# Issuing the stores of gathered blocks' results from ACT in place of SP

## What is computed

```python
x = layernorm(x + attn(x))        # attention in windows of 128 tokens over this and the previous window, v = k
x = layernorm(x + ffn(x))
# ffn: rotary positions, then causal attention over 2048 tokens, 16 heads of 16
q, k, v = q_in @ Wq.T + bq, k_in @ Wk.T + bk, x @ Wv.T + bv
attn = softmax(where(causal, q @ k.T / 4, -inf)); ctx = attn @ v
x1 = layer_norm(x + ctx @ out_proj_w.T + out_proj_b, ln1)
gates = softmax(x1 @ gate_w.T + gate_b); top_gates, top_idx = top_k(gates, 2)   # 8 experts
moe_out = sum of the two chosen (x1 @ expert_w[e].T + expert_b[e]) * gate
return layer_norm(x1 + moe_out, ln2)
```

## Time and profile before

| | |
|---|---|
| time, median of 3 runs | 1423.48 us (1422.62 to 1425.06) |
| the profiled execution | 1425.19 us, its span 1423.5 us |
| busy share of PE, DVE, ACT, POOL | 94%, 75%, 57%, 40% |
| granted TensorE clock, mean | 0.977 of 2.4 GHz |
| bytes moved | 140.77 MB, mean 99 GB/s |
| transfers issued by SP | all but the gathers and scatters of Pool |

### The profile page before, as it was taken

The page is one execution under the profiler, slowest core; times in us unless marked ns, Lnnn a source line. Parts: engine busy times, 40 slices in busy tenths (PEclk is TensorE's granted clock), DMA queues, the critical chain, the costliest instruction groups (busy, mean ns, idle before and its releaser), DMA issues. The chain is left out here.

```text
span 1423.5 us, 29390 instructions
## 1 busy us (share of the span) xinstructions
PE 1334.6 (94%) x9678; PEld 766.4 (54%) x9678; DVE 1072.4 (75%) x2782; ACT 805.4 (57%) x1749; POOL 572.1 (40%) x806
## 2 busy tenths in 40 slices
PE   8889899999999999999979888999999999999984
PEld 6767655545554453556656545665433445665441
DVE  3665877987888977674559977786999886666776
ACT  3235366556666567676745455656656666666541
POOL 4434422221221532223558645343454023322786
PEclk9999999999999999999989999999989999999996
DMA  3765432232111423445375543554432123443331
GB/s 113 191 179 130 123 79 62 62 91 57 40 40 47 95 58 92 110 117 147 89 181 135 133 85 74 163 166 136 109 77 63 29 48 67 131 125 104 89 73 46
DMA packets 221665, 140.77 MB, mean 99 GB/s; under 512 B 130246, under 2 KB 215934, under 8 KB 221259
## 3 DMA queue, kind: packets, MB, share of 16 engines
q1 hardware_dynamic: 209755, 123.50, 32.7%
q0 software_dynamic: 11760, 15.40, 5.6%
HBM read 97.35 MB, written 40.88 MB: 97 GB/s over the span
## 5 line engine op out<-in xcount | busy, mean ns | idle before, releaser
L1320 DVE TENSOR_REDUCE mxs<-bank 128x1 f32<-128x512 f32 (+3 forms) x1120 | 712.5, 667 | 169.2 <-PE bank L1753 95.6
L1213 ACT ACTIVATE pbuf<-bank 128x512 f32<-128x512 f32 (+1 forms) x1112 | 599.0, 593 | 296.3 <-PE bank L1804 187.7
L1781 PE MATMUL bank<-qs,ks 99*128 99x256 bf16 (+3 forms) x1536 | 426.5, 321 | 16.4 <-DVE rD L1445 6.8
L1753 PE MATMUL bank<-ks,qs 96*128 96x512 bf16 (+3 forms) x1280 | 423.3, 351 | 4.0 <-DVE mxs L1320 1.3
L1804 PE MATMUL bank<-pbuf,vcur 128*17 128x256 f32 (+3 forms) x3072 | 274.0, 474 | 9.1 <-DMA vcur<-v_scratch 7.0
L1781 PEld LDWEIGHTS bank<-qs,ks 99*128 99x128 bf16 x1536 | 142.2, 98 | 192.0 <-issue 69.4
L1753 PEld LDWEIGHTS bank<-ks,qs 96*128 96x128 bf16 x1280 | 123.1, 98 | 111.3 <-issue 21.3
L1804 PEld LDWEIGHTS bank<-pbuf,vcur 128*17 128x17 f32 x3072 | 70.8, 97 | 140.1 <-issue 97.4
L1125 POOL DMA_INDIRECT gathering<-x_scratch,gathering x69 | 68.3, 990 | 182.1 <-PE bank L1928 158.5
L1136 POOL DMA_INDIRECT gathering<-ys_scratch,gathering x48 | 78.8, 1641 | 46.9 <-issue 18.1
L1079 POOL CAST parts<-qkf 128x512 bf16<-128x512 f32 x28 | 17.7, 632 | 175.3 <-DVE qkf L1414 175.2
(11 more groups left out here) (334 smaller groups left out, 1941.6 us busy)
## 6 DMA issues: line engine op xcount, KB each, us to landing
gathering<-exp_t SPq DMA_DIRECT2D x69, 256.0 KB
vcur<-v_scratch SPq DMA_DIRECT2D x92, 136.0 KB, 2.8
parts_scratch<-parts SPq DMA_DIRECT2D x29, 384.0 KB, 3.4
ys_scratch<-gathering SPq DMA_DIRECT2D x69, 128.0 KB, 3.2
xw<-windows SPq DMA_DIRECT2D x29, 256.0 KB, 3.4
x_scratch<-x SPq DMA_DIRECT2D x53, 128.0 KB, 2.4
qs<-parts_scratch SPq DMA_DIRECT2D x32, 192.0 KB, 3.8
ks<-parts_scratch SPq DMA_DIRECT2D x28, 192.0 KB, 3.8
```

The lines of the kernel that those rows point to most:

```text
L1213: nc.scalar.activation(pbuf[:, u0:u0 + heads, nj * P - cols:nj * P], bk[:, 0:heads * cols].rearrange("p (h t) -> p h t", h=heads), ACT.Exp)\
L1320: v.reduce_max(mxs[:, j * HJ + h:j * HJ + h + heads, c], bk[:, 0:heads * cols].rearrange("p (h t) -> p h t", h=heads), AX_X)\
L1753: last = mm(bk[:, x * cols:(x + 1) * cols].rearrange("p (n t) -> p n t", t=P), qs6[0:KR, pos % QRING, head // HJ, j, head % HJ, :], ks5[0: ...
L1781: last = mm(bk[:, x * cols:(x + 1) * cols].rearrange("p (n t) -> p n t", t=P), ks5[0:KR + NPART, kslot, kb % GT, head, :], qs6[0:KR + NPAR ...
```

## The change

The step `s_st` moves from SP to ACT: the same transfer of the same slot to the same place, with the same semaphore, is issued in ACT's stream. There it waits until ACT's own `s_ec` has finished. In the planner its engine becomes ACT, its cost 150 ns in place of 900, it loses the 640 ns (5 x 128) of wire and SP's settling of 1700 ns, and gains 3000 ns in `INDIRECT` and ACT's settling of 150.

```diff
-INDIRECT = {"s_g": 3600, "b_g1": 4000, "b_g2": 5000, "t_sc": 3600}
+INDIRECT = {"s_g": 3600, "b_g1": 4000, "b_g2": 5000, "t_sc": 3600, "s_st": 3000}
...
-                    add("s_st", u + x, "SP", 900, ("s_ec", u + x))
+                    add("s_st", u + x, "ACT", 150, ("s_ec", u + x))
...
-                elif name == "s_st":
-                    u, t = T, T % BLOCKS
-                    sp.wait_ge(*drain("s_e", u))
-                    sp.dma_start(ys_dram[u // BLOCKS][t * P:(t + 1) * P, :], yslot[u % 2]).then_inc(yslot_stored[u % 2], 16)
...
+                elif name == "s_st":
+                    u, t = T, T % BLOCKS
+                    act.wait_ge(*drain("s_e", u))
+                    act.dma_start(ys_dram[u // BLOCKS][t * P:(t + 1) * P, :], yslot[u % 2]).then_inc(yslot_stored[u % 2], 16)
```

## The result

The changed kernel takes 1430.49 us by the median of 18 runs (1424.7 to 1436.47), the kernel before 1423.05 in 18 runs of its own (1416.98 to 1428.59). The ratio is 1.0048, with a 95% interval of 1.0033 to 1.0064: slower by 7 us. The profiled execution took 1428.72 us with a span of 1427.0, the one of before 1425.19 with 1423.5. So the two traces show 3.5 us of the 7; single executions of one kernel lie up to 0.4% from its median, so a difference of a few us between two whole traces may be chance.

A forecast was written before the change was run, and what follows sets the result against it. The prediction took TensorE, busy 94% of the span, to bound the kernel. Its terms, 0 + 0 + 2 + 0 = +2 us, gave 1425.5 us from a usual run's 1423.5; the range was 1414 to 1436.

The forecast's parts named there:

- What bounds the kernel: TensorE, busy 94% of the span; only 3.1 us idle in the three store phases; gain taken as 0, at most −3.1.
- its part of the chain: In the chain that ended last, TensorE's part ends at 1336.1 us; what follows is Pool's with DVE's.
- The landing: Stores land after 3.2 us, 1.7 without a load before; up to 1.5 us gain at phase ends, taken as 0.
- What comes to ACT: ACT's time for issuing 69 stores: from nothing to 42 us, against 148.5 us of its idle time in the phases.
- The upper end of 0.61 us a store: ACT's most for each store: 0.11 us of lost overlap, 0.03 for the semaphore, 0.47 for the issue.
- The 12 us pushed back: ACT time delayed by the 69 stores: half at 0.1 us each, half at 0.26 us each.
- What reaches TensorE: Of the 12 us pushed back on ACT, one part in six delays TensorE: +2 us.
- first rival: ACT's slip empties the three `st` banks, whose cover is 0.3 us, and reaches TensorE: 10 us, 1433.5 us; chance 0.25.
- The order: New planner costs change bank hand-out and all five engines' orders after about 545 us: 0, with −8 to +8 us.
- third rival: The new order makes one more long wait of TensorE: +7 us, 1430.5 us; chance 0.10.
- The sign that I gave for the order: TensorE's idle changing by more than 5 us in 686 to 856 or behind 1312 us would show the order.

The follow-up runs named there:

- e8: Changed kernel with ACT's list swapped at 30 places, so one activation stands between copy and store; 1428.94 us, ratio 1.0040 to the kernel before.
- e1: Changed kernel with the planner of the kernel before: old order and banks, the 69 stores issued by ACT; 1426.79 us, ratio 0.9995.
- e12: e1 with the planner's cost of a store 800 in place of 900 ns, giving e11's order with stores on ACT; 1456.57 us, ratio 0.9989.
- e11: Kernel before, stores still on SP, only the planner's cost of a store set to 800 in place of 900 ns; 1418.96 us, ratio 0.9969.
- e6: Order of the kernel before, stores issued by ACT in two halves of 64 partitions each; 1479.4 us, ratio 1.0130.
- e9: Changed kernel, but the planner gets the new costs for the third chunk's stores alone; 1429.13 us, ratio 1.0030 to the kernel before.
- e10: Changed kernel, but the planner gets the new costs for the first two chunks' stores alone; 1427.49 us, ratio 1.0031 to the kernel before.
- e3: Changed kernel with the store's landing in the planner 3100 in place of 3000 ns, another order; 1433.74 us, ratio 1.0054.
- e2: Kernel before with the changed kernel's planner: new order and banks, stores still issued by SP; 1428.13 us, ratio 1.0014.
- e4: The changed kernel itself, run again on another chip beside e5; 1465.24 us, ratio 1.0044 to the kernel before.
- e5: The same kernel as e2 (new order, stores on SP), run again beside the changed kernel; 1462.18 us, ratio 1.0032.

## Why the prediction was right in its range and not in its likeliest case

I forecast 1425.5 us as the likeliest and no change as the likeliest of the three, with 1414 to 1436 as the range and 0.35 for slower. It came out at 1430.5, which is slower, above the 1426.3 at which I let no change end. Step by step:

- **What bounds the kernel.** Right for the phases with the stores: they have 3.1 us of idle to give, and nothing was given (3.6 us now). No run shows a gain from SP's freed time or the earlier landing. Wrong for the end: I let TensorE end at 1336 us, where its part of the chain ends. But it is busy for 82.05 us of the last 112, and its last matmul ends at 1404.7, so the last stage had TensorE's work in it for the new order to move.
- **The landing.** The open question, 3.2 us or 1.7, is answered: 1.8 where ACT issues, 3.2 where SP does, in both orders. The stores had stood behind the 256 KB of weights ahead of them. The rule of the Trainium skill ("DMA: Bandwidth & Descriptors", section "Issuing engines are not separate DMA queues"), that transfers of different issuers run on the same 16 DMA engines and a second issuer saves only the sequencer's time, fits e8: a store on ACT's own queue right behind the weights lands after 3.2 us as well. What I drew from it, a gain of 0, was wrong: the 1.4 us come from the store being started ahead of the load. That nobody waits for it was right as far as the times show.
- **What comes to ACT.** The upper end of 0.61 us a store was too high: 0.33 for the issue and 0.04 for the wait, and nothing in the case shown beside an exponential. The 12 us pushed back were probably too many; no run gives that figure. The Trainium skill's picture of a sequencer held to the end of the record ("Perfetto Trace Analysis", "DMA Instruction — HWDGE (DVE, Sync)") is compatible with this only because the activation ahead still computes meanwhile: at 1206.52 the sequencer is held, the engine is not.
- **What reaches TensorE.** +2 us was the term; with the order kept, e1 measures −0.7 us with ±2.3, and e12 beside e11 about +3. The first rival's 0.3 us of cover was not measured: the limit lies between what is absorbed (0.33, partly overlapped) and what isn't (1.1 and more, e6). Its price of 10 us for this change was too high; that the issue is shorter than I took it from SP is one reason.
- **The order.** This is the step that was mis-sized. I put the term at 0 with ±8 us; it is +3.3 us by the mean of two measurements of the order alone (0.23% of 1423), and 4.3 and 4.4 us by e9 and e10, with the move in them. The third rival, that the new order makes a wait more, comes nearest to what happened. That its figure, 1430.5, is the measured one is luck: its chance was put at 0.10, the order explains 3 to 5 of its 7 us, and the traces show not one long wait but a later third phase and a later end of TensorE's work. The sign that I gave for the order, a change of idle by more than 5 us in 686 to 856 or behind 1312, failed: it changed by 0.3 and 1.6 us.
- **Where the sign stood.** I had written that the sign can't be read from the trace of before. It could be read from the plan, which is made before the kernel is built. By the planner's own times TensorE's last step starts at 1418.3 us in the order of before and at 1424.7 in the changed one, and the third chunk's first gather comes 327.2 and 331.8 us after the second's. The plan puts that last step at 1428.0 for e3, 1426.1 for e9 and 1417.8 for e10 and e11. TensorE's last matmul in the traces ends at 1404.7 us (before), 1411.1 (changed), 1412.7 (e2), 1413.5 (e3), 1415.0 (e9), 1403.0 (e10) and 1396.9 (e11): later or earlier as planned each time, though not by the planned amount. One trace is a rough witness, since e1, which has the plan of before, ends it at 1408.7; and the plan is no full forecast, as e10 is 0.31% slower all the same. I also called the first stores some tenths of a us earlier in the plan; the very first is 1.6 us earlier.
- **Open.** The changed kernel's 1.0046 less the order's 1.0023 leaves 3 us. The 3.1 us between e4 and e5 tie them to the issue by ACT in the new order, and none of the runs shows through which wait they would arise. The move in a list with more stores directly behind their copies (30 of 69, 20 in e1) is a candidate; e8 took those away and came out at 1.0040, which decides nothing.

## What to carry to other kernels

In a kernel whose order a planner makes, a change of engine is two changes: run it once in the old order, and once more the new order without it, before believing either. And compare the two plans first: here the new one already had TensorE's last step 6.4 us later. Here the order alone was worth −0.3% (e11) to +0.3% (e5), with every instruction as it was, and a plain variation of one cost gave the faster version (e11, 0.9969) that the move had been unable to give. A store issued from the engine that makes its data cost nothing here where another instruction of that engine covered the issue; look how long the engine is held, and how much the consumer of its next result has in store. When a transfer lands late, look at what was started just ahead of it, on any queue.

## What the runs showed of the hardware

An issue of 128 partitions of 1 KB takes 0.326 us on ACT (69 times, 0.400 at most, the changed kernel) and 0.467 on SP by the median; of 64 partitions it takes 0.570 us on ACT by the median, more than the whole (e6). An activation that has been started goes on under the issue behind it (1206.39 to 1206.98 us of the changed kernel). A store of 128 KB within 1 us behind a load of 256 KB landed after 3.2 us by the median, from SP's queue (61 stores, before) and from ACT's (7, e8) alike; the others landed after 1.8 and 2.0. And 12 matmuls that took 5.32 us at a granted clock of 1.00 took 6.76 at 0.79, right behind a wait of TensorE.
